# Reordered start-up loads, an interleaved first chunk and casts split over two engines in an eight-core Mamba, feed-forward and attention kernel

## The reference

```python
x = x + mamba(_layernorm(x), W_in, conv_w, W_x, W_dt, b_dt, W_Bp, D_param, W_out)
x = x + ffn(_layernorm(x), w_gate, w_up, w_down)
x = x + attn(_layernorm(x), W)
x = x + ffn(_layernorm(x), w_gate, w_up, w_down)

# mamba: xc, z = split(x @ W_in)             W_in [1024, 4096]
#        u  = silu(causal_conv(xc, 4 taps))
#        dt_raw, B_raw = split(u @ W_x)      W_x [2048, 32]
#        dt = clip(softplus(dt_raw @ W_dt + b_dt), 1e-4, 1); ub = u * (B_raw @ W_Bp)
#        h_t = h_(t-1) * (1 - dt_t) + ub_t   scan over the tokens
#        out = ((h + D_param * u) * silu(z)) @ W_out     W_out [2048, 1024]
# ffn:   int32 weights / 127; h = silu(x @ wg.T) * (x @ wu.T); out = h @ wd.T
# attn:  causal softmax of x against K, plus x itself; K, V = split(x @ W.T)
```

## Time and profile before

| | us |
|---|---|
| median of two runs | 3461.66 (3442.72 and 3480.59) |
| profiled execution, its own time | 3324.74 |
| its span on the slowest core (core 6) | 3323.2 |
| spans of the eight cores | 3292.9 to 3323.2 |

### The profile page before, as it was taken

One profiled execution on the slowest core, in us unless ns is written; L12 is line 12 of the kernel. 1 busy time (PEld: TensorE's weight loads), 2 busy tenths in 40 slices (PEclk: granted clock), 3 DMA queues, 4 the chain that ended last, 5 costly groups with the idle time before them and its releaser, 6 DMA issues.

```text
span 3323.2 us, 29901 instructions; the slowest of 8 cores (3292.9 to 3323.2 us)
## 1 busy us (share of the span) xinstructions
PE 1981.7 (60%) x9274; PEld 974.9 (29%) x9432; DVE 954.7 (29%) x1617; ACT 776.6 (23%) x1196; POOL 323.6 (10%) x404
## 2 busy tenths in 40 slices
PE   0355555555555531285676759514988486859587
PEld 0233333333333310131332324212444232324232
DVE  3244444444444441010211211153343121211121
ACT  0244545445454423300111101010011200101010
POOL 0222222122222210013000000000000000000000
PEclk9576666776667755698788889856998698989889
DMA  7200000000000017615112030343031512030303
GB/s 248 76 14 26 1 26 1 26 26 1 26 1 26 16 42 247 211 54 185 34 54 73 28 99 8 126 160 116 1 133 57 187 38 89 16 111 0 121 7 98
DMA packets 69851, 233.31 MB, mean 70 GB/s; under 512 B 8450, under 2 KB 8578, under 8 KB 67652
## 3 DMA queue, kind: packets, MB, share of 16 engines
q10 hardware_dynamic: 35712, 112.21, 10.0%
q1 hardware_dynamic: 27460, 91.92, 9.0%
q0 software_dynamic: 6528, 27.27, 2.0%
HBM read 170.55 MB, written 60.82 MB: 70 GB/s over the span
## 4 chain that ended last, share of the span: by engine, by line
PE 37%; DMA 22%; DVE 13%; ACT 9%; issue 8%; DVEq 4%; POOLq 3%; POOL 2%; ACTq 2%; SPq 0%
PE ps_s L975 15%; DMA arena<-wd_c 7%; PE ps_s L941 5%; DVEq L143 4%; DMA arena<-xs 4%; PE ps_s L1045 3%; PE ps L1045 3%; POOLq L143 3%; ACT L679 2%; POOL arena L560 2%; PE ps_s L1297 2%; DVE arena L516 2%; PE ps L759 2%; PE ps_s L1223 2%; DMA arena<-wu_t 2%
## 5 line engine op out<-in xcount | busy, mean ns | idle before, releaser
L975 PE MATMUL ps_s<-arena 128*128 128x512 bf16 x2256 | 505.6, 385 | 10.8 <-DVE arena L328 8.6
L584 PE MATMUL ps_s<-arena 128*128 128x256 bf16 x1024 | 214.1, 397 | 339.2 <-ACT arena L508 336.8
L318 PE MATMUL ps<-arena 128*128 128x128 bf16 x512 | 63.4, 306 | 486.0 <-DVE arena L307 486.0
L975 PEld LDWEIGHTS ps_s<-arena 128*128 128x128 bf16 x2304 | 227.7, 99 | 287.3 <-issue 23.8
L1045 PE MATMUL ps_s<-arena 128*128 128x512 bf16 x752 | 207.0, 395 | 140.3 <-DMA arena<-wd_c 89.9
L266 ACT ACTIVATE arena<-arena 128x1024 bf16<-128x1024 f32 x64 | 67.6, 1057 | 908.2 <-DMA arena<-xs 817.9
L584 PEld LDWEIGHTS ps_s<-arena 128*128 128x128 bf16 x1024 | 136.6, 138 | 409.4 <-issue 356.2
L941 PE MATMUL ps_s<-arena 128*128 128x512 bf16 x752 | 172.6, 390 | 122.7 <-ACT arena L951 61.2
L499 PE MATMUL ps_s<-arena 128*128 128x256 bf16 x1024 | 173.3, 342 | 109.8 <-DVE arena L447 61.7
L990 DVE TENSOR_TENSOR arena<-arena,ps_s 128x512 bf16<-128x512 f32 x144 | 99.0, 688 | 421.5 <-ACT arena L984 421.5
L1045 PE MATMUL ps<-arena 128*128 128x512 bf16 x752 | 207.4, 396 | 1.0 <-issue 0.2
(11 more groups left out here) (93 smaller groups left out, 2398.0 us busy)
## 6 DMA issues: line engine op xcount, KB each, us to landing
xs<-arena ACTq DMA_DIRECT2D x48, 512.0 KB, 2.9
arena<-xs ACTq DMA_DIRECT2D x48, 512.0 KB, 4.2
arena<-wd_c SPq DMA_DIRECT2D x84, 256.0 KB, 2.6
arena<-wd_c ACTq DMA_DIRECT2D x84, 256.0 KB, 2.6
arena<-wg_t SPq DMA_DIRECT2D x16, 768.0 KB, 7.0
arena<-wu_t SPq DMA_DIRECT2D x16, 768.0 KB, 6.5
arena<-x ACTq DMA_DIRECT2D x16, 512.0 KB, 4.5
arena<-w_in ACTq DMA_DIRECT2D x8, 1024.0 KB, 9.7
```

The source lines that it names most:

```text
L318: lambda e, s=xn_bf_tile, dj=dj, pbf=pbf: e.transpose(pbf[:, dj * P:(dj + 1) * P], s[:, dj * P:(dj + 1) * P], g_ident),
L584: lambda e, dj=dj, ci=ci, bkx=bkx, half=half, par=par: e.matmul(psb[bkx][:, half * TCM:(half + 1) * TCM], win_bf[:, dj * 4096 + ci * P: dj ...
L975: lambda e, hi=hi, dj=dj, bk=bk, par=par, wsrc=wsrc: e.matmul(psb[bk], wsrc[:, dj * H + hi * P: dj * H + (hi + 1) * P], fxnt[par][:, dj * ...
```

## The change

Three edits:

1. The small-weights block (w_x, w_dt, w_bp, memset) is moved behind the w_in loop and ahead of the w_out loop, on VectorE's list and on SP's.
2. In the first chunk xc and z pairs alternate, as in the later chunks.
3. In the first feed-forward the casts of slot 1 (every second tile) are made by VectorE, and wait in addition for ACT's cast of the tile before.

```diff
         mamba_load_ln(0)
         mamba_transpose(0, [mk_sm_all, mk_sm_all])
 
-        em.op("vector", lambda e: e.tensor_copy(
-            wx_bf[:], wx_stage[:, 0:512]), wait=[mk_sm], inc=[(s_ve, 1)],
-            drain=False)
-        mk_wx = s_ve.mark()
...
-        mk_ones = s_ve.mark()
-
         win_bf = VA(M_WIN, 65536, BF16)
...
                 mk_win_cast[dj] = chain[slot] = s_ve.mark()
+
+        em.op("vector", lambda e: e.tensor_copy(
+            wx_bf[:], wx_stage[:, 0:512]), wait=[mk_sm], inc=[(s_ve, 1)],
+            drain=False)
+        mk_wx = s_ve.mark()
...
+                w = [prevc] if prevc else []
+                mkd = dma("sync", stage[0:nrow, 0:1024],
+                          srcw[:, hh * 1024:(hh + 1) * 1024], sd_g1, wait=w)
...
+        mk_ones = s_ve.mark()
 
         wout_bf = VA(M_WOUT, 32768, BF16)
...
         for p in range(8):
             phaseA_xc_pair(0, p)
-        for zp in range(8):
-            phaseA_z_pair(0, zp)
+            phaseA_z_pair(0, p)
         mk_xz_last = s_pe.mark()
...
-                            prev2[slot] = mkk[dj] = s_se.mark()
+                            ceng = "scalar" if slot == 0 else "vector"
+                            csem = s_se if slot == 0 else s_ve
+                            if slot == 0:
+                                em.op("scalar",
...
+                            else:
+                                em.op("vector",
+                                      lambda e, dj=dj, hh=hh, dstw=dstw, slot=slot: e.tensor_copy(
+                                          dstw[:, dj * H + hh * 1536: dj * H + (hh + 1) * 1536],
+                                          stg[slot][:]),
+                                      wait=[mkd, prev2[0]], inc=[(s_ve, 1)],
+                                      drain=False)
+                            prev2[slot] = mkk[dj] = csem.mark()
```

More of the change, by code:

```diff
@@ L452, in build_nc @@
                 mk_win_cast[dj] = chain[slot] = s_ve.mark()
+        em.op("vector", lambda e: e.tensor_copy(
+            wx_bf[:], wx_stage[:, 0:512]), wait=[mk_sm], inc=[(s_ve, 1)],
+            drain=False)
+        mk_wx = s_ve.mark()
+        mk_wx_stage = mk_wx
+        prevc = None
+        for m, (srcw, dstw, nrow) in enumerate(
+                ((w_dt, wdt_bf, 17), (w_bp, wbp_bf, 16))):
+            for hh in range(2):
+                w = [prevc] if prevc else []
+                mkd = dma("sync", stage[0:nrow, 0:1024],
+                          srcw[:, hh * 1024:(hh + 1) * 1024], sd_g1, wait=w)
+                em.op("vector",
+                      lambda e, dstw=dstw, hh=hh, nrow=nrow: e.tensor_copy(
+                          dstw[0:nrow, hh * 1024:(hh + 1) * 1024],
+                          stage[0:nrow, 0:1024]),
+                      wait=[mkd], inc=[(s_ve, 1)], drain=False)
+                prevc = s_ve.mark()
+        mk_wdtbp = prevc
+        em.op("vector", lambda e: e.memset(xpd_bf[0:32, :], 1.0),
+              inc=[(s_ve, 1)], drain=False)
+        mk_ones = s_ve.mark()
         wout_bf = VA(M_WOUT, 32768, BF16)
@@ L896, in ffn @@
                                       sd_wa if slot == 0 else sd_wb, wait=w)
[L897 to L901, removed]
-                            prev2[slot] = mkk[dj] = s_se.mark()
+                            ceng = "scalar" if slot == 0 else "vector"
+                            csem = s_se if slot == 0 else s_ve
+                            if slot == 0:
+                                em.op("scalar",
+                                      lambda e, dj=dj, hh=hh, dstw=dstw, slot=slot: e.copy(
+                                          dstw[:, dj * H + hh * 1536: dj * H + (hh + 1) * 1536],
+                                          stg[slot][:]),
+                                      wait=[mkd], inc=[(s_se, 1)], drain=False)
+                            else:
+                                em.op("vector",
+                                      lambda e, dj=dj, hh=hh, dstw=dstw, slot=slot: e.tensor_copy(
+                                          dstw[:, dj * H + hh * 1536: dj * H + (hh + 1) * 1536],
+                                          stg[slot][:]),
+                                      wait=[mkd, prev2[0]], inc=[(s_ve, 1)],
+                                      drain=False)
+                            prev2[slot] = mkk[dj] = csem.mark()
                             prev_cast[0] = mkk[dj]
```

## The result

The changed kernel took 3307.5 us (median of its runs), the kernel before 3331.6 in the same measurement. The ratio, after to before, is 0.9948 with an interval of 0.9934 to 0.9963: 17 us less, between 12 and 22. A later measurement of the same two kernels gave 0.9958 [0.9942, 0.9974]. Both are under 2%, which counts as no change here. The ratio leaves out, for both kernels, the runs in which the cores of one die had a lower granted clock (0.72 to 0.78 instead of 0.79 to 0.80) and the time was some 3 to 6% longer, and so it shows less than the 24 us between the medians; the two runs that stood ahead of the prediction, 3442.7 and 3480.6, lie among these by their times, though their cores are not on record. The profiled execution of the changed kernel took 3300.4, that of the kernel before 3324.7.

What follows compares the result with a forecast made beforehand. The prediction saw a loop of waits, not a full engine, in the places changed; 4.3 + 6.5 + 2.6 = 13.4 us off the two runs' median of 3461.7 gave 3448 us, range 3300 to 3487.

Steps and rivals of the forecast that it cites:

- Part 1: Start-up, small-weights block behind w_in: 16.0 us gained in w_in, 11.7 given back before w_out, 4.3 us net.
- if that cast ends after 115, part 1 failed: Sign in the profile after: the last w_out cast was to come near 111 us; ending after 115 meant failure.
- Part 2: First chunk, xc and z in turn: 6.9 us a pair, gaining 6.5 us (9 at 6.5 a pair, 1.2 at 7.8).
- rival of the low clock: First chunk: TensorE stays at 1.2 GHz, so the xc/z edit gives 1.2 and the sum is 8 us; chance 0.15.
- Part 3: Feed-forward weights, every second cast on VectorE: 3.6 - 2.5 + 1.5 = 2.6 us gained, between 10.2 gained and 5.5 lost.
- (c): Weight stage: an odd cast takes 0.96 us on VectorE instead of 1.47 on ACT, gaining 1.5 us.
- (a): End of weight stage: table load, silu and gate matmuls wait only for ACT's even casts, starting 3.6 us earlier.
- (b): Start of weight stage: the first odd cast stands behind the normalisation in VectorE's list, costing 2.5 us.
- rivals of round trips: Weight stage bound by its two slots' load-and-cast round trips: 9.3 us gained there, sum 20; chance 0.15.
- collisions: Weight stage: VectorE casts and GpSimd's stores hold each other up, 14 us lost, sum 2 slower; chance 0.08.
- start-up rival: Start-up: w_in comes only 11 us earlier, the gap before w_out eats it and 0.7 more; sum 8.4; chance 0.12.
- Wrong if a stage outside changes by over 5 us: Stages outside the three edits: the prediction is wrong if one changes its length by over 5 us.

Runs made afterwards that it cites:

- dt_split: The changed kernel with each w_dt half loaded as two transfers, row 16 alone and rows 0 to 15; 3313.1 us in one execution.
- p1_only: The kernel before with only the small-weights block moved behind w_in; ratio to before 0.9999 [0.9967, 1.0031].
- p2_only: The kernel before with only xc and z pairs alternating in the first chunk; ratio to before 0.9967 [0.9950, 0.9983].
- first_act: The changed kernel with the first odd weight cast back on ScalarE, the other fifteen on VectorE; 3316.2 us in one execution.
- best: The changed kernel with small loads ahead of w_in, w_dt halves split 16+1 rows, four w_out slots, first odd cast on ScalarE; 3283.2 us, ratio to before 0.9891.
- p3_only: The kernel before with only the odd weight casts moved to VectorE; ratio to before 0.9998 [0.9979, 1.0017].
- after_again: The changed kernel measured once more, beside best; ratio to before 0.9958 [0.9942, 0.9974].

## Why the prediction was right or wrong

**The absolute time was wrong by 140 us, and the step that failed is the last sentence of the sum**, "against the median of the two runs ... the same 13.4 us give 3448". The profiled execution, 3324.7, was the one to build on: all eleven runs of before, those two among them, have a median of 3331.6, and the nine new ones 3325.1, within 0.2% of it. The two lay 3.5 and 4.7% above the profiled execution of the same program; I widened the range to hold both and then put the forecast on the wrong side. The same 13.4 us out of the profiled execution gave 3311.3, 4 us from the 3307.5 measured. The range, 3300 to 3487, holds the result; "within 2%" was the right class.

**Part 1, forecast 4.3, measured 1.8 in the profiled pair and 0.6 alone.** The gain was right: w_in 16.0 earlier forecast, 16.2 and 15.5 measured. What is given back was too small: 11.7 forecast, 14.8 measured. The term that was mis-sized is "each later half is a round trip of 2.84 us", taken from w_bp with 16 rows for w_dt with 17. On the core shown, the spacing of the w_dt casts is 68.75 - 63.65 = 5.10, 2.3 more, and the row of before with 5.79 us of wait for this very load had been there to read. In the medians, the end of the last w_in cast and the first w_out issue are 9.6 us apart, 7.1 forecast, and that issue and the last cast's start 41.7, 42.6 forecast: 1.6 over together (1.8 by the loops, 52.2 against 50.4). The other 1.3 of the 3.1 is the side of before: the core read for the prediction had a loop of 38.7, the median core 37.4. dt_split takes some 2 back by the split of one row alone. Whether part 1 gives anything at all the runs don't tell: the five kernels with this start-up end w_out at 116.4 in the mean, the three without the edit at 117.5, and the five alone scatter by 3.7; the ratio of p1_only is 0.9999, within 0.3% either way. The criterion "if that cast ends after 115, part 1 failed" stands half: 114.6 and 114.4 in the two executions of the changed kernel, 117.5 to 118.1 in the three others.

**Part 2, forecast 6.5, measured 9.6** (mean of 62.6, 61.9 and 61.9 without the edit against 52.2 to 52.9, mean 52.5, with it), 0.6 over the upper end. The mechanism was right (ACT's round plus a z silu), the term mis-sized is the 6.9 us a pair: five of the six spacings on the core shown are 6.43, the first 7.14 (copies at 124.06 and 131.20). The six make 39.3 us instead of 41.4. That is 2.1 of the 2.3 us by which the cores shown (61.9 and 53.1, 8.8 apart) are over the forecast; the rest of the 9.6 is that the median cores differ a little from these. The reason for taking more than 6.5 was the clock, and it mostly doesn't fall between the bursts as I feared. Rows 6 had shown the rise after 4 us without a gap; that the upper level can hold through a gap, a row of the xc pairs of before showed, which I hadn't used:

```profile
138.00:140.00 2.00, 0.00 (x0) 0.00 (x0) 0.00 (x0) 0.77 (x2) 1.08 (x1) 1.00 0.00 0
```

That it is mostly kept with 32 matmuls a round (0.95 in the mean of the stage, against 0.58 with 16), no row of before showed. The rival of the low clock is out, by p2_only and by every kernel with the edit.

**Part 3, forecast 2.6, measured 2.8** (mean 154.5 without, 151.7 with). (c) was priced from a float cast at 0.96, and the int32 cast took 0.96. (a) is seen directly: the gate silu at 1375.38 beside the VectorE cast at 1375.29, ahead of that cast's end, with the last ACT cast at 1372.60. (b) is seen in order (1252.62, then 1253.23); its price, 2.5, has 2 us from first_act and best as its only measurement. The marks split the 2.8 further. From the end of the last Mamba chunk to the last even cast's start are 148.3 us in the three kernels without the edit, 149.0 in the seven with it and 146.9 in first_act and best (means of the medians). So (b) and (c) together cost 0.7, where 1.0 was forecast, which leaves 3.5 to (a), 3.6 forecast; (b) alone is 2.1 and (c) gives 1.4, 1.5 forecast. The seven scatter by 3 us, so this is a reading of the split and no proof. The rivals of round trips (for the odd slot) and of collisions fell as shown above. The rule of the Trainium skill that the prediction cites (SBUF — State Buffer, section "SBUF: two separate sides") stood against this part. The trace agrees with it in the issue: 1.12 us beside the normalisation, as before the change, and 1.15 beside an odd cast on core 3 of p3_only. It cost the stage nothing that can be seen.

**The sum**: 1.2 (the middle of 1.8 and 0.6, and not to be told from nothing) + 9.6 + 2.8 = 13.6 by the marks, 13.4 forecast. That is luck in part: 3 too much in part 1 and 3 too little in part 2. The ratios say 14 and 17, and those of the three parts alone add up to 12 (0.0001 + 0.0033 + 0.0002, of 3330). The start-up rival (nothing gained because w_in comes only 11 earlier) is wrong in its mechanism and nearly right in its size. The bounds of the three parts add up to 5 us lost and not to 6, which moves nothing.

**"Wrong if a stage outside changes by over 5 us"**: the rest went from 1929.1 to 1922.7, 6.4 less, in the profiled pair. The experiments don't bear this out as an effect of the change: after_again has 1928.5 with the same code, and the other kernels 1928.8 to 1939.6. The criterion was set tighter than two single executions can tell. What in the rest scatters by 17 us from execution to execution I haven't followed.

## What to carry to other kernels

Price a transfer by one of the same shape, best by its own row in the trace of before: here 17 rows cost twice what 16 did, its row of 5.79 us stood unused, and held back whatever came behind them on the queue, which a split into 16 and 1 removed. When a serial chain is moved behind a stream, count what had been loaded ahead under that stream's end: the block gave back 15 of the 16 us that moving it won, while loading its data early and keeping four tiles in flight gained 22 us at the same place. Before a time is forecast, look whether the profiled execution and the timed runs agree; if they lie per cents apart, say which of the two is the base and why.

## What the runs showed of the hardware

- A transfer of 17 rows of 4 KB with nothing else in flight took 4.2 to 5.4 us of waiting on the cores of the five kernels with the changed start-up, one of 16 rows 2.1 to 2.4; with the 17 rows ahead of 128-row tiles on the queue, the DMA share was 0.07 (27 GB/s) for 4 us and a tile issued at 5.97 was cast at 27.53.
- TensorE with 32 matmuls of 256 columns per 6.43 us was granted 1.00 for most of the stage, through gaps of 2.8 us, 0.95 in the mean of 131 to 163 us; with 16 per 5.92 us it was at 0.50 for most of it and 0.58 in the mean of 128 to 164 us in the kernel before. 16 matmuls took 1.91 us and 3.57 us.
- An int32 to bf16 cast of 128x1536 took 0.96 us on VectorE and 1.47 on ScalarE.
- GpSimd's issue of a store took 0.53 us alone, 1.12 to 1.13 beside the normalisation on VectorE and 1.15 beside an int32 cast on VectorE, which kept its 0.96 us.
